# Attention edges of a graph network kernel: rows normalised on ScalarE, silu taken directly, one cross product over all channels, biases as a ones row, six filler products

## The chip, the cores and the metric

The kernel is one program on one core of a Trainium2 chip. The metric is the device time of a whole launch in microseconds (us), lower is better. The core has TensorE (PE: matmuls, with PEld its weight loads), VectorE (DVE), ScalarE (ACT), GpSimd (POOL) and SyncE (SP, which here only issues DMAs). Each engine runs its own instructions in the order in which they were written; engines wait for one another by semaphores. Everything is float32.

## The reference, cut to what matters

Three graph layers and a fourth with attention run on 100,000 nodes of 160 numbers (64 scalars and 32 vectors of 3) and 25,000 edges. The change lies in the part of the fourth layer that runs over the edges:

```
s, v = eq_ln(node)                      # rows of both ends of an edge, normalised
ms = s[src] @ msrc_ws + s[dst] @ mdst_ws + mdst_bs
mv = the same for the vectors
h  = silu(ln(edge_scalars @ rw1 + rb1, rg1, rbe1))      # radial network
h  = silu(ln(h @ rw2 + rb2, rg2, rbe2))
w1..w5 = split(h @ rw3 + roff)
Y1 = sqrt(3) * rhat                     # unit vector of the edge
ds = [w1 * ms, w4 * (mv . Y1) / sqrt(3)]
dv = [(w2 * ms) Y1, w3 * mv, w5 * cross(mv, Y1) / sqrt(2)]
ls, lv = ds @ lin_ws + lin_bs, dv @ lin_wv
alpha, values = first 64 of ls, (last 64 of ls, lv)
logit = sum over each head of smooth_leaky(alpha) * alpha_dot
```

Outputs of this part, for each edge: the logits (8 heads), the values (160), and the normalised row of its destination.

## The kernel before, in words

The program runs phases one after the other, with a barrier between: weights, all nodes, an edge index, three edge layers, `attention_weights`, `attention_edges` (L1653 to L2165), a softmax, and the destination nodes. Only `attention_weights` and `attention_edges` are changed.

`attention_edges` takes 25,000 edges in 25 rounds of 4 lanes; a lane holds J = 2 tiles of P = 125 edges (W = 250 columns when turned). There are thus 100 lane passes, and "a pass" below is the work of one lane, or the stretch of time in which each engine does each step once. Lane n owns the PSUM banks 2n and 2n+1.

The list `order` gives each step a position, `part` (17.05) the distance from lane to lane. `run_rounds` sorts the steps of the four lanes by position modulo 4 * part, and writes them for each engine in that order; so within a pass an engine's steps follow one another by position modulo `part`, and steps of three or four different edge lanes are interleaved. Nothing is reordered at run time.

The steps of a lane, in order of data: `load` (SP), `measure` to `widen` (DVE: statistics of the gathered rows), `roots` (POOL: a power, L1785), `divide` and `normalize` (DVE: L1868 to L1883), `turn_src`, `turn_dst` (PE transposes) with `copy_src`, `copy_dst` (ACT). Beside it the radial network, twice: `hidden` (PE), `h_add`, `h_measure`, `h_merge`, `h_widen` (DVE), `h_roots` (POOL, L1792), `h_normalize` (DVE), `turn_h` (PE), `activate` (ACT: the affine value and the tanh of half of it), `h_gate` (DVE: their product, a silu). Then `turn_vec`, `spread_vec` (PE) with ACT copies, `linear` (PE), `copy_linear` (ACT), `weights` (PE), `products`, `product4` (DVE), `outputs` (PE, 8 matmuls), `bias` (DVE), `copy_values`, `take_tanh` (ACT), `cross0` to `cross2` (DVE, 18 instructions of 32 elements, L1966), `leak`, `leaked`, `dot`, `add_heads` (DVE), `store` (SP). `keep_attr` (ACT) frees the row for `gather_next` (POOL): an index copy (L1761) and four indirect DMAs (L1768) that fetch the rows of the lane's next round.

`keep_busy0` to `keep_busy4` are steps of PE alone: 3, 2, 5, 3 and 3 matmuls of the identity (L127) whose results nobody reads. In the profile each float32 matmul leaves two records; so these 16 fillers are 32 records of L127 in a pass. A transpose leaves one record.

Of the kernel before, what the change touches and what calls it, by code (L numbers as in the profile page):

```python
# [7 lines left out]
ALU = mybir.AluOpType  # L8
# [5 lines left out]
P = 125  # L14
J = 2
# [1524 lines left out]
def attention_weights(nc, sem, keep, sb, banks, inp, w):  # L1540
# [45 lines left out]
    for name, src in (("lin_4", thrice(g["lin_ws"][S:S + U, :])),  # L1586
                      ("rb1", g["rb1"].unsqueeze(0).broadcast_to([P, 64])),
                      ("rb2", g["rb2"].unsqueeze(0).broadcast_to([P, 64])),
                      ("lin_b", g["lin_bs"].unsqueeze(0).broadcast_to([P, 128])),
                      ("alpha_dot", g["alpha_dot"].rearrange("h k -> (h k)").unsqueeze(0).broadcast_to([P, 64])),  # L1590
                      ("roff12", g["roff"][0:128].unsqueeze(1))):
        loads.append((w[name][:, :], src))
# [11 lines left out]
    with nc.Block() as block:  # L1604
# [6 lines left out]
        def _(v):  # L1611
            for x in ("src_s", "dst_s", "rw1", "rw2", "rw3", "proj_s", "spread"):
                v.memset(w[x][:, :], 0.0)
# [12 lines left out]
            kron(v, w["lin_5"], lin_5, 1.5 ** 0.5)  # L1626
            kron(v, w["proj_v"], proj_v, 1.0)
            v.tensor_copy(w["lin_a"][0:S, 0:128], lin_s[:, :])
            v.tensor_scalar(w["lin_a"][S:128, 128:160], lin_v0[S:128, :], 3 ** 0.5, None, ALU.mult)
# [3 lines left out]
            v.tensor_scalar(w["rw2"][0:64, :], rw2[:, :], 0.5, None, ALU.mult)  # L1633
            v.tensor_scalar(w["rw3"][0:64, 0:128], rw3[:, 0:128], 0.5, None, ALU.mult)
            for k in range(3):
                v.tensor_scalar(w["rw3"][0:64, 128 + k * V:128 + (k + 1) * V].rearrange("p (u c) -> p u c", c=3),
                                rw3[:, 128 + k * U:128 + (k + 1) * U].unsqueeze(2).broadcast_to([64, U, 3]),
                                0.5, None, ALU.mult)
            v.tensor_scalar(w["rg"][:, 2:4], w["rg"][:, 0:2], 0.5, None, ALU.mult)
            v.tensor_scalar(w["rbe"][:, 2:4], w["rbe"][:, 0:2], 0.5, None, ALU.mult).then_inc(built, 1)  # L1640
# [12 lines left out]
def attention_edges(nc, sem, sb, banks, inp, w, e, index, table, kept, logits, edges):  # L1653
# [7 lines left out]
    radial = [["h_added" + k, "h_measured" + k, "h_merged" + k, "h_widened" + k, "h_normed" + k, "h_gated" + k]  # L1661
              for k in ("1", "2")]
    t = lane_steps(sem, "att",
              pe=["attr_turned", "hidden1", "src_turned", "h_turned1", "dst_turned", "hidden2", "h_turned2",
                  "vec_turned", "vec_spread", "linear", "weights", "outputs"],
              act=["attr_copied", "src_copied", "h_activated1", "dst_copied", "attr_kept", "h_activated2",
                   "vec_copied", "spread_copied", "linear_copied", "values_copied", "tanh"],
              dve=["measured", "merged", "differences", "squares", "summed", "widened", *radial[0][:4], "x3",
                   "normed", *radial[0][4:], *radial[1], "products", "product4", "biased",
                   *[f"cross{k}" for k in range(3)], "leak", "leaked", "dotted", "logits"],  # L1670
              pool=["roots", "h_roots1", "h_roots2"])

    part = 17.05
    order = [("load", 0.0), ("turn_attr", 2.7), ("measure", 2.7), ("copy_attr", 3.3), ("merge", 4.25),
             ("differences", 4.95), ("hidden1", 5.2), ("squares", 5.4), ("add_squares", 5.65), ("widen", 5.85),
# [8 lines left out]
             ("copy_vec", 25.4), ("spread_vec", 26.0), ("keep_busy4", 26.46), ("copy_spread", 26.8),  # L1684
             ("linear", 27.4), ("copy_linear", 29.45), ("weights", 31.4), ("products", 33.45),
             ("product4", 34.9), ("outputs", 37.05), ("bias", 40.1), ("copy_values", 41.55),
             ("take_tanh", 41.95), ("cross0", 46.55), ("cross1", 47.75), ("cross2", 48.95), ("leak", 53.0),
             ("leaked", 53.35), ("dot", 53.65), ("add_heads", 55.2), ("store", 55.65)]

    fill = [(3, 1, 3), (1, 0, 2), (0, 0, 5), (0, 0, 3), (0, 0, 3)]  # L1690
# [4 lines left out]
    index_copied = [sem(f"att_index_copied_lane{n}") for n in range(LANES)]  # L1695
# [15 lines left out]
    h_u = sb("att_h_u", [64, LANES, W])  # L1711
    h_tanh = sb("att_h_tanh", [64, LANES, W])
    p5 = sb("att_p5", [V, LANES, W])
    keep = sb("att_keep", [P, T, KEPT + 1])
    alpha = sb("att_alpha", [P, LANES, J, 64])
    tanh = sb("att_tanh", [P, LANES, J, 64])
    logit = sb("att_logit", [P, T, HEADS])

    with nc.Block() as block:
        @block.sync  # L1720
        def _(sp):
# [3 lines left out]
            def load(n, i):  # L1725
# [3 lines left out]
                sp.wait_ge(t["dve"][n], count_at(t, i, "dve", "x3"))  # L1729
# [7 lines left out]
            def store(n, i):  # L1737
                sp.wait_ge(t["dve"][n], count_at(t, i + 1, "dve", "logits"))
                gate(sp, t)
                sp.wait_ge(t["act"][n], count_at(t, i + 1, "act", "attr_kept"))  # L1740
                gate(sp, t)
# [13 lines left out]
        def _(p):  # L1755
            prime(p, t, "pool")

            def gather(n, i):

                own = slice(J * n, J * n + J)  # L1760
                p.tensor_copy(e["ends_now"][:, :, own], index["ends"][:, :, bass.ds(i * T + J * n, J)]  # L1761
                              ).then_inc(index_copied[n], 1)
                p.wait_ge(index_copied[n], i + 1)
                gate(p, t)
# [7 lines left out]
            def gather_next(n, i):  # L1772

                p.wait_ge(gathered[n], 64 * i + 64)
                gate(p, t)
                p.wait_ge(t["dve"][n], count_at(t, i + 1, "dve", "normed"))
# [3 lines left out]
                gather(n, i + 1)  # L1780
# [14 lines left out]

            for n in range(LANES):
                gather(n, 0)
# [6 lines left out]
        def _(v):  # L1804
            for x in (e["attr_t"], e["h"], e["h2"], r_t):
                v.memset(x[:, :, :], 0.0)
            v.memset(keep[:, :, ATTR + 1:KEPT + 1], 0.0).then_inc(cleared, 1)
            prime(v, t, "dve")
# [54 lines left out]
            def divide(n, i):  # L1863

                v.wait_ge(t["pool"][n], count_at(t, i + 1, "pool", "roots"))
                v.wait_ge(kept_stored[n], 48 * i + 48)
                for j in range(J):
                    v.tensor_scalar(keep[:, J * n + j, X3:X3 + X], e["rows"][:, n, 1, j, 0:X],  # L1868
                                    e["rows"][:, n, 1, j, MEAN:MEAN + 1], root[:, n, 8 + j:9 + j], ALU.subtract, ALU.mult)
                    v.tensor_scalar(r[:, n, 0, j, :], e["y"][:, J * n + j, 0:3], root[:, n, 10 + j:11 + j], None,  # L1870
                                    ALU.mult)
                    ins = v.tensor_scalar(r[:, n, 1, j, :], e["y"][:, J * n + j, 0:3], root[:, n, 10 + j:11 + j],
                                          -1.0, ALU.mult, ALU.mult)
                one(ins, n)

            def normalize(n, i):
                for j in range(J):
                    for side, x in enumerate((e["xs"], e["xd"])):
                        k = side * J + j
# [758 lines left out]
```

## Time and profile before

| | |
|---|---|
| median of 3 runs | 11330.98 us (11328.65 to 11331.06) |
| the profiled execution, its own time | 11326.82 us |
| its span, first to last instruction | 11325.1 us |
| mean granted TensorE clock of the span | 0.88 of full |
| busy share of the span | PE 80%, PEld 73%, DVE 72%, ACT 40%, POOL 47% |
| `attention_edges` in the span | about 8122 to 10056 us |

Busy shares are averages over phases of different kinds; what bounds the changed phase is read in that phase. In the profile's rows a duration is that of one instruction from start to end; neighbours on an engine overlap a little, so the distance from start to start is shorter. PEclk 1.00 is the upper of the two clock levels of TensorE (2.4 GHz), 0.50 the lower (1.2 GHz).

### The profile page before, as it was taken

The numbers are of one execution on the slowest core, as the hardware profiler recorded it, in microseconds if no ns is written. First come the engines' busy times: TensorE is split into PE (matmuls) and PEld (weight loads), VectorE is DVE, ScalarE is ACT, GpSimd is POOL, SyncE is SP. The second block draws the span as 40 slices with busy tenths as digits, with TensorE's granted clock in tenths as the row PEclk, the third lists the DMA queues.
The fourth block names the chain that finished last, engine by engine and source line by source line (L and its number), as shares of the span: only waits on it lengthen the run. The fifth ranks groups of instructions, "written<-read, shape, count | busy, mean of one in ns | idle before, by whom it ended". The sixth has DMA issues, their size and how long they took to land. (4 is left out here: it accounts for less than half of the span.)

```text
span 11325.1 us, 241587 instructions
## 1 busy us (share of the span) xinstructions
PE 9089.1 (80%) x58771; PEld 8291.2 (73%) x58771; DVE 8098.2 (72%) x40535; ACT 4475.4 (40%) x17107; POOL 5279.8 (47%) x6680
## 2 busy tenths in 40 slices
PE   7877787777778787799978887888588888849998
PEld 6777777777777777688866676777577777738888
DVE  5666666666666666688878887888688888877777
ACT  4555555555555555333322232333222222212222
POOL 3444444444444444577755554555444444423444
PEclk8888888888888888899999998999888888869999
DMA  2222222222222222233322222222111111111111
GB/s 68 85 86 85 85 86 85 86 86 85 86 86 85 86 85 85 70 77 77 77 63 68 68 67 59 57 57 57 39 40 40 39 39 40 39 32 51 53 54 48
DMA packets 988491, 753.89 MB, mean 67 GB/s; under 512 B 430970, under 2 KB 948478, under 8 KB 988048
## 3 DMA queue, kind: packets, MB, share of 16 engines
q1 hardware_dynamic: 823696, 587.78, 18.4%
q0 software_dynamic: 164352, 162.20, 6.0%
q14 instruction: 409, 3.35, 0.1%
q8 instruction: 34, 0.56, 0.0%
HBM read 362.41 MB, written 392.80 MB: 67 GB/s over the span
## 5 line engine op out<-in xcount | busy, mean ns | idle before, releaser
L749 ACT ACTIVATE nodes_x<-nodes_z 125x161 f32<-125x161 f32 x2400 | 1005.5, 422 | 1439.1 <-DVE nodes_z L673 1437.4
L127 PE MATMUL bank<-ident 128*128 128x128 f32 x10000 | 1478.0, 297 | 97.1 <-PEq L883 58.7
L127 PEld LDWEIGHTS bank<-ident 128*128 128x128 f32 x10000 | 1415.1, 213 | 145.5 <-issue 59.2
L814 PE MATMUL bank<-self_v,nodes_v_t 128*125 128x98 f32 x4800 | 1153.2, 328 | 0.0
L812 PE MATMUL bank<-self_s,nodes_s_t 128*125 128x65 f32 x4800 | 977.2, 291 | 150.9 <-DVE ffn_y L233 143.6
L812 PEld LDWEIGHTS bank<-self_s,nodes_s_t 128*125 128x125 f32 x4800 | 879.8, 223 | 226.6 <-issue 206.4
L612 POOL TENSOR_SCALAR nodes_z<-nodes_sum 125x2 f32<-125x2 f32 x400 | 113.2, 283 | 1987.4 <-DVE nodes_sum L663 1987.4
L673 DVE SCALAR_TENSOR_TENSOR nodes_z<-bank,nodes_z 125x162 f32<-125x162 f32 x2400 | 811.2, 380 | 273.7 <-PE bank L814 271.4
L1203 POOL DMA_INDIRECT table<-edge_new,edge_into_now x600 | 733.5, 1222 | 565.5 <-issue 516.4
L312 PE MATMUL bank<-ident,ffn_sn 125*65 125x125 f32 x800 | 264.6, 346 | 788.3 <-DVE ffn_sn L214 784.3
L663 DVE TENSOR_REDUCE nodes_sum<-nodes_z 125x2 f32<-125x322 f32 x400 | 195.4, 489 | 948.8 <-DMA nodes_z<-rows 948.8
L814 PEld LDWEIGHTS bank<-self_v,nodes_v_t 128*125 128x125 f32 x4800 | 865.6, 226 | 0.0
L1171 POOL DMA_INDIRECT edge_rows<-table,edge_ends_now x416 | 519.6, 1249 | 598.0 <-DVE edge_carry L1056 532.2
L312 PEld LDWEIGHTS bank<-ident,ffn_sn 125*65 125x65 f32 x800 | 134.9, 169 | 839.1 <-issue 836.3
L1437 ACT ACTIVATE edge_sums<-bank 125x163 f32<-125x163 f32 x600 | 151.3, 304 | 1282.8 <-PE bank L1525 1282.8
L1171 POOL DMA_INDIRECT edge_rows<-rows,edge_ends_now x416 | 505.0, 1214 | 220.7 <-DVE edge_carry L1056 123.5
L1768 POOL DMA_INDIRECT att_edge_rows<-table,att_edge_ends_now x416 | 511.0, 1228 | 194.0 <-POOL att_edge_ends_now L1761 97.9
L233 DVE SCALAR_TENSOR_TENSOR ffn_y<-bank,nodes_z,nodes_u 125x160 f32<-125x160 f32 x800 | 270.3, 379 | 414.0 <-issue 220.1
L1288 DVE SCALAR_TENSOR_TENSOR edge_msg<-bank,edge_y,edge_msg 125x65 f32<-125x65 f32 x1800 | 510.0, 283 | 32.0
L795 PE MATMUL bank<-ident,nodes_z 125*65 125x125 f32 x1600 | 510.3, 334 | 1.4 <-DVE nodes_z L673 1.3
L796 PE MATMUL bank<-ident,nodes_z 125*97 125x125 f32 x1600 | 503.7, 331 | 0.0
L338 PE MATMUL bank<-f_v,ffn_hid_v 128*125 128x160 f32 x1600 | 478.3, 390 | 0.0
(496 smaller groups left out, 30563.3 us busy)
## 6 DMA issues: line engine op xcount, KB each, us to landing
table<-nodes_z SPq DMA_DIRECT2D x1200, 160.2 KB
nodes_z<-rows SPq DMA_DIRECT2D x400, 160.2 KB
out<-nodes_res SPq DMA_DIRECT2D x400, 156.2 KB
nodes_v_t<-x_t SPq DMA_DIRECT2D x400, 94.7 KB
edge_dst_row<-dst SPq DMA_DIRECT2D x300, 122.1 KB
ordered<-edge_new SPq DMA_DIRECT2D x200, 160.2 KB
edge_rows<-ordered SPq DMA_DIRECT2D x200, 160.2 KB
dest_rows<-kept SPq DMA_DIRECT2D x100, 316.4 KB
```

What stands on the lines that cost most here:

```text
L127: pe.matmul(banks[2 * ((n + lead) % LANES) + odd][:, 0:128], w["ident"][:, :], w["ident"][:, :], start=True, stop=True)
L338: ins = pe.matmul(b[0:P, o:o + F], f["hid_v2"][:, n, c], f["w"]["f2_v2"][:, :], start=False, stop=True, skip_group_check=True)
L673: ins = v.scalar_tensor_tensor(z[:, l + 1, k, 0:A + 1], banks[2 + n % 2][0:P, o:o + A + 1], z[:, l, k, A:A + 1], z[:, l, k, 0:A + 1], ALU. ...
L749: ins = act.activation(x3[:, k, :], z[:, l + 1, k, 0:X], ACT.Square, bias=z[:, l + 1, k, MEAN:MEAN + 1], scale=-1.0, accum_out=total[:, l, ...
L795: pe.transpose(banks[n % 2][0:S + 1, j * P:(j + 1) * P], z[:, l, k, 0:VS], ident)
L796: ins = pe.transpose(banks[n % 2][0:V + 1, W + j * P:W + (j + 1) * P], z[:, l, k, MEAN:X], ident)
L812: pe.matmul(banks[2 + n % 2][0:P, o:o + VS], xs[:, n, c], w[f"self_s{l}"][:, :], start=True, stop=True)
L814: ins = pe.matmul(banks[2 + n % 2][0:P, o + MEAN:o + A + 1], xv[:, n, c], w[f"self_v{l}"][:, :], start=False, stop=True, skip_group_check= ...
L1171: p.indirect_dma_start(e["rows"][:, n, side, j, :], None, source, bass.IndirectOffsetOnAxis(ap=e["ends_now"][:, side, k:k + 1], axis=0)).t ...
L1203: p.indirect_dma_start(target, bass.IndirectOffsetOnAxis(ap=e["into_now"][:, k:k + 1], axis=0), e["new"][:, n, j, :], None, bounds_check=n ...
L1288: v.scalar_tensor_tensor(scalars, bank[0:P, o:o + 1 + S], y, scalars, ALU.mult, ALU.add)
L1768: p.indirect_dma_start(e["rows"][:, n, side, j, :], None, table, bass.IndirectOffsetOnAxis(ap=e["ends_now"][:, side, k:k + 1], axis=0)).th ...
```

## The change

- `part` is 13.00 and every position in `order` is new. The fillers `keep_busy` go; instead `linear` issues six identity matmuls after its own four.
- `divide` and `normalize` of DVE become `offsets` on DVE (five small instructions: the unit vector with its first two components repeated, and minus mean times root for ten rows) and `normalize` on ACT: ten Identity activations with a bias and a scale per partition (four of 64, four of 96 and two of 161 columns).
- `activate` is one Silu instead of an Identity and a Tanh; `h_gate` goes. The radial bias becomes a row of ones in the operand and a row in the weights; `h_add` goes, and `h_measure` and `h_normalize` read PSUM.
- The output bias likewise; `bias` goes. `copy_values`, `take_tanh` and `cross0` wait for `outputs` itself. `outputs` has ten matmuls: a separate one of 32 columns, and one of 160 columns (5 per channel) in place of 96.
- The cross product: three multiplications and three additions over 125x192 elements (`cross0` to `cross3`) for 18 instructions. `leak` and `leaked` become one instruction.
- The index copy goes from POOL to ACT (`keep_attr`), with the wait for the gathered rows; `gather_next` is the four indirect DMAs.

```diff
-    part = 17.05
+    part = 13.00
+    order = [("load", 0.0), ("measure", 5.54), ("merge", 7.7), ("turn_attr", 9.71), ("copy_attr", 10.22),
+             ("differences", 10.3), ("hidden1", 10.63), ("squares", 10.87), ("h_measure1", 11.21),
+             ("add_squares", 11.46), ("widen", 11.68), ("roots", 11.9), ("offsets", 13.74), ("normalize", 14.31),
+             ("h_merge1", 14.36), ("h_widen1", 14.66), ("h_roots1", 14.9), ("h_normalize1", 15.66),
+             ("turn_h1", 16.16), ("activate1", 16.76), ("turn_src", 16.96), ("hidden2", 17.31),
+             ("copy_src", 17.61), ("h_measure2", 17.89), ("h_merge2", 18.3), ("h_widen2", 19.67),
+             ("h_roots2", 19.9), ("keep_attr", 20.08), ("gather_next", 20.52), ("turn_dst", 20.77),
+             ("copy_dst", 21.42), ("h_normalize2", 21.48), ("turn_h2", 22.04), ("activate2", 22.55),
+             ("turn_vec", 23.07), ("copy_vec", 23.58), ("spread_vec", 23.99), ("copy_spread", 24.6),
+             ("linear", 25.01), ("copy_linear", 26.54), ("weights", 27.23), ("products", 29.01),
+             ("product4", 30.38), ("outputs", 30.8), ("cross0", 32.75), ("cross1", 33.53), ("copy_values", 33.7),
+             ("take_tanh", 34.07), ("cross2", 34.3), ("cross3", 34.83), ("leak", 35.19), ("dot", 35.52),
+             ("add_heads", 35.84), ("store", 36.18)]
...
+            def offsets(n, i):
+                v.wait_ge(t["pool"][n], count_at(t, i + 1, "pool", "roots"))
...
+                v.tensor_tensor(r[:, n, :, 0:3], y[:, :, 0:3], scale.broadcast_to([P, J, 3]), ALU.mult)
+                v.tensor_tensor(r[:, n, :, 3:5], y[:, :, 0:2], scale.broadcast_to([P, J, 2]), ALU.mult)
+                v.scalar_tensor_tensor(offset[:, n, 0:4].unsqueeze(2), mom[:, n, 0, :, 0:1], -1.0,
+                                       root[:, n, 0:4].unsqueeze(2), ALU.mult, ALU.mult)
...
+            def cross0(n, i):
+                v.wait_ge(t["pe"][n], count_at(t, i + 1, "pe", "outputs"))
+                along, plus, minus = three(n)
+                v.tensor_tensor(along, vectors_of(n)[:, :, 0:U].unsqueeze(3).broadcast_to([P, J, U, 3]),
+                                turned_r(n, 0), ALU.mult)
+                v.tensor_tensor(plus, wide_of(n, 1), turned_r(n, 2), ALU.mult)
+                one(v.tensor_tensor(minus, wide_of(n, 2), turned_r(n, 1), ALU.mult), n)
...
             def activate(k):
                 def step(n, i):
                     wait("pe", n, i, f"h_turned{k + 1}")
-                    x = banks[2 * n + 1][0:64, 0:W]
-                    act.activation(h_u[:, n, :], x, ACT.Identity, bias=w["rbe"][:, k:k + 1],
-                                   scale=w["rg"][:, k:k + 1])
-                    one(act.activation(h_tanh[:, n, :], x, ACT.Tanh, bias=w["rbe"][:, 2 + k:3 + k],
-                                       scale=w["rg"][:, 2 + k:3 + k]), n)
+                    one(act.activation(e[("h", "h2")[k]][0:64, n, :], banks[2 * n + 1][0:64, 0:W], ACT.Silu,
+                                       bias=w["rbe"][:, k:k + 1], scale=w["rg"][:, k:k + 1]), n)
...
+            def normalize(n, i):
+                wait("dve", n, i, "offsets")
+                act.wait_ge(kept_stored[n], 48 * i + 48)
+                for j in range(J):
+                    for side, x in enumerate((e["xs"], e["xd"])):
+                        k, row = side * J + j, e["rows"][:, n, side, j, :]
+                        act.activation(x[:, n, j, 0:S], row[:, 0:S], ACT.Identity, bias=offset[:, n, k:k + 1],
+                                       scale=root[:, n, k:k + 1])
+                        act.activation(x[:, n, j, S:F], row[:, VS:X], ACT.Identity, bias=offset[:, n, 4 + k:5 + k],
+                                       scale=root[:, n, 4 + k:5 + k])
+                    ins = act.activation(keep[:, J * n + j, X3:X3 + X], e["rows"][:, n, 1, j, 0:X], ACT.Identity,
+                                         bias=offset[:, n, 8 + j:9 + j], scale=root[:, n, 8 + j:9 + j])
+                one(ins, n)
...
             def linear(n, i):
...
                 one(pe.matmul(a[0:V, W:2 * W], w["dst_v"][:, :], e["dv_t"][0:V, n, :], start=False, stop=True), n)
+                for _ in range(6):
+                    pe.matmul(banks[2 * n + 1][:, 0:128], w["ident"][:, :], w["ident"][:, :], start=True, stop=True)
...
-                    pe.matmul(bank[0:P, 0:160], e["p01"][:, n, c], w["lin_a"][:, :], start=True, stop=True)
...
+                    pe.matmul(heads[:, j, 0:128], e["p01"][:, n, c], w["lin_a"][:, :], start=True, stop=True)
+                    pe.matmul(heads[:, j, 0:128], p4[:, n, c], w["lin_4"][:, :], start=False, stop=True,
+                              skip_group_check=True)
+                    pe.matmul(heads[:, j, 128:224], e["p2"][:, n, c], w["lin_3"][:, :], start=True, stop=True)
+                    pe.matmul(vectors[:, j, 0:U], e["p01"][:, n, c], w["lin_sv"][:, :], start=True, stop=True)
+                    ins = pe.matmul(vectors[:, j, U:6 * U], p5[:, n, c], w["lin_5"][:, :], start=True, stop=True)
```

## Rows read from the trace of the kernel before

**Rows 1.** Windows, the loop of `attention_edges`: busy us (x instructions) per engine, PEclk, DMA.
```profile
8210.00:10010.00 1800.00, 1454.34 (x8612) 1289.46 (x8611) 1514.43 (x8404) 516.17 (x1632) 839.05 (x764) 0.84 0.18 39
```

**Rows 2.** Source line 1743, SP's store of a pass: ns min/median/max, first and last start.
```profile
L1743 SPq FUSED_REGOPS  x96: 37/51/74, 8225.0 to 10013.5; - x96
```

**Rows 3.** Timeline of POOL, one pass: start, us, engine, line, operation, [idle before].
```profile
9027.95 0.18 POOL L1761 COPY att_edge_ends_now<-edge_ends 125x4 int32 x1 [6.81 <-ACT att_keep L2030]
9029.08 1.28 POOL L1768 DMA_INDIRECT att_edge_rows<-table,att_edge_ends_now  x1 [0.95 <-POOL att_edge_ends_now L1761]
...
9034.91 0.75 POOL L1792 TENSOR_TENSOR att_h_root<-att_h_wide,half 125x2 f32<-125x2 f32 x1
9036.68 2.27 POOL L1785 TENSOR_TENSOR att_root<-att_wide,half 125x12 f32<-125x12 f32 x1 [1.02 <-DVE att_wide L1860]
...
9045.21 0.19 POOL L1761 COPY att_edge_ends_now<-edge_ends 125x4 int32 x1 [5.60 <-ACT att_keep L2030]
```

**Rows 4.** Lines of the phase, shapes apart, of ACT and DVE: busy us, mean ns.
```profile
L2015 ACT ACTIVATE att_h_u<-bank,att_rbe,att_rg 64x250 f32<-64x250 f32 x200 | 111.1, 556 | 766.4 <-PE bank L2105 766.4
L2009 ACT ACTIVATE att_edge_attr_t<-bank 64x250 f32<-64x250 f32 x100 | 37.3, 373 | 209.1 <-PE bank L2082 164.4 <-DVE att_keep L1807 44.6
L2050 ACT ACTIVATE att_keep<-bank 125x96 f32<-125x96 f32 x200 | 37.0, 237 | 7.2 <-DVE att_keep L1949 7.2
L1966 DVE SCALAR_TENSOR_TENSOR att_keep<-bank,att_r,att_keep 125x32 f32<-125x32 f32 x1800 | 322.7, 256 | 7.6 <-ACT att_keep L2050 0.5
L1882 DVE TENSOR_SCALAR att_edge_xs<-att_edge_rows,att_root 125x96 f32<-125x96 f32 x200 | 65.3, 327 | 0.0
L1891 DVE TENSOR_TENSOR att_hx<-bank,att_rb 125x128 f32<-125x128 f32 x200 | 56.2, 281 | 1.1 <-PE bank L2093 1.1
L1948 DVE TENSOR_TENSOR att_alpha<-bank,att_lin_b 125x64 f32<-125x64 f32 x200 | 43.7, 218 | 1.1 <-PE bank L2158 1.1
```

**Rows 5.** Timeline of ACT in the node phase: two Identity activations with bias and scale.
```profile
1007.09 0.93 ACT L759 ACTIVATE nodes_res<-ffn_y,nodes_out_offset,ffn_y_root 125x160 f32<-125x160 f32 x2
```

**Rows 6.** Timeline of all engines, one pass, parts of it.
```profile
9002.75 1.04 PE L2129 MATMUL bank<-att_r_t,att_spread 96*96 96x250 f32 x2
...
9010.26 0.48 DVE L1931 SCALAR_TENSOR_TENSOR att_edge_p<-bank,att_roff,att_edge_f 128x250 f32<-128x250 f32 x1 [1.27 <-PE bank L2148]
...
9012.48 0.51 PE L2154 MATMUL bank<-att_lin_a,att_edge_p 128*125 128x160 f32 x2 [1.66 <-DVE att_edge_p L1942]
...
9014.01 0.22 DVE L1825 BATCH_NORM_STATS2 att_stats<-att_edge_rows 125x6 f32<-125x64 f32 x1
...
9014.16 0.44 PE L2158 MATMUL bank<-att_lin,att_p 96*125 96x96 f32 x2
...
9015.46 0.18 DVE L1834 BATCH_NORM_AGGREGATE att_moments<-att_stats 125x2 f32<-125x6 f32 x1
...
9015.96 0.15 DVE L1835 BATCH_NORM_AGGREGATE att_moments<-att_stats 125x2 f32<-125x6 f32 x1
```

**Rows 7.** Timeline of PE, another pass, parts of it.
```profile
9036.53 0.37 PE L2105 MATMUL bank<-ident,att_hn 125*64 125x125 f32 x2 [2.67 <-DVE att_hn L1915]
...
9039.02 0.63 PE L2129 MATMUL bank<-att_r_t,att_spread 96*96 96x250 f32 x2
...
9042.80 0.84 PE L127 MATMUL bank<-ident 128*128 128x128 f32 x6
...
9044.03 0.59 PE L2145 MATMUL bank<-att_edge_h,att_rw 128*128 128x250 f32 x2
...
9046.11 0.62 PE L2093 MATMUL bank<-att_rw,att_edge_h 128*125 128x64 f32 x4 [0.23 <-DVE att_edge_h L1922]
```

**Rows 8.** Windows of three stretches after `outputs` of Rows 6; columns as in Rows 1.
```profile
9014.50:9018.00 3.50, 1.86 (x9) 1.56 (x8) 2.95 (x27) 0.00 (x0) 2.36 (x3) 0.50 0.26 64
9018.10:9020.90 2.80, 2.80 (x14) 2.60 (x15) 2.16 (x13) 1.47 (x5) 2.69 (x2) 0.50 0.45 110
9021.20:9026.00 4.80, 4.80 (x35) 4.35 (x33) 4.76 (x25) 1.83 (x6) 0.00 (x0) 1.00 0.09 13
```

More of the change, by code:

```diff
@@ L1660, in attention_edges @@
     logit_view = logits.rearrange("(t p) h -> p t h", p=P)
-    radial = [["h_added" + k, "h_measured" + k, "h_merged" + k, "h_widened" + k, "h_normed" + k, "h_gated" + k]
-              for k in ("1", "2")]
-    t = lane_steps(sem, "att",
[L1664 to L1671, printed above, removed]
@@ L1673, in attention_edges @@
-    part = 17.05
-    order = [("load", 0.0), ("turn_attr", 2.7), ("measure", 2.7), ("copy_attr", 3.3), ("merge", 4.25),
-             ("differences", 4.95), ("hidden1", 5.2), ("squares", 5.4), ("add_squares", 5.65), ("widen", 5.85),
[8 rows of a table removed]
[L1684 to L1688, printed above, removed]
@@ new lines, in attention_edges @@
+    done = {"pe": {"turn_attr": "attr_turned", "hidden1": "hidden1", "hidden2": "hidden2", "turn_src": "src_turned",
+                   "turn_dst": "dst_turned", "turn_h1": "h_turned1", "turn_h2": "h_turned2", "turn_vec": "vec_turned",
+                   "spread_vec": "vec_spread", "linear": "linear", "weights": "weights", "outputs": "outputs"},
+            "act": {"copy_attr": "attr_copied", "normalize": "normed", "copy_src": "src_copied",
+                    "copy_dst": "dst_copied", "activate1": "h_activated1", "activate2": "h_activated2",
+                    "keep_attr": "attr_kept", "copy_vec": "vec_copied", "copy_spread": "spread_copied",
+                    "copy_linear": "linear_copied", "copy_values": "values_copied", "take_tanh": "tanh"},
+            "dve": {"measure": "measured", "merge": "merged", "differences": "differences", "squares": "squares",
+                    "add_squares": "summed", "widen": "widened", "offsets": "offsets", "products": "products",
+                    "product4": "product4", "cross0": "cross0", "cross1": "cross1", "cross2": "cross2",
+                    "cross3": "cross3", "leak": "leaked", "dot": "dotted", "add_heads": "logits"},
+            "pool": {"roots": "roots", "h_roots1": "h_roots1", "h_roots2": "h_roots2"}}
@@ L1756, in _, with gather @@
             prime(p, t, "pool")
[L1758 to L1764, printed above, removed]
+            def gather(n):
                 for j in range(J):
@@ new lines, in cross1, with cross2, cross3 @@
+            def cross1(n, i):
+                after(i, n, "cross0")
+                along, plus, minus = three(n)
+                one(v.tensor_tensor(plus, plus, minus, ALU.subtract), n)
+            def cross2(n, i):
+                after(i, n, "cross1")
+                along, plus, minus = three(n)
+                one(v.tensor_tensor(plus, plus, along, ALU.add), n)
+            def cross3(n, i):
+                after(i, n, "cross2")
+                v.wait_ge(t["act"][n], count_at(t, i + 1, "act", "tanh"))
+                gate(v, t)
+                v.wait_ge(kept_stored[n], 48 * i + 48)
+                gate(v, t)
+                one(v.tensor_tensor(keep[:, J * n:J * n + J, S:F],
+                                    heads_of(n)[:, :, 128:224],
+                                    three(n)[1].rearrange("p j w c -> p j (w c)"), ALU.add), n)
@@ L1991, in _ @@
                 measure=measure, merge=merge, differences=differences, squares=squares, add_squares=add_squares,
-                widen=widen, divide=divide, normalize=normalize, **radial_steps("1"), **radial_steps("2"),
-                products=products, product4=product4, bias=bias, cross0=cross(0), cross1=cross(1), cross2=cross(2),
-                leak=leak, leaked=leaked, dot=dot, add_heads=add_heads))
+                widen=widen, offsets=offsets, **radial_steps("1"), **radial_steps("2"),
+                products=products, product4=product4, cross0=cross0, cross1=cross1, cross2=cross2, cross3=cross3,
+                leak=leak, dot=dot, add_heads=add_heads))
         @block.scalar
@@ L2028, in keep_attr @@
             def keep_attr(n, i):
-                wait("dve", n, i, "x3")
-                one(act.activation(keep[:, J * n:J * n + J, ATTR + 1:ATTR + 2], e["rows"][:, n, 1, :, A:A + 1],
-                                   ACT.Copy), n)
+                act.wait_ge(gathered[n], 64 * i + 64)
+                gate(act, t)
+                act.wait_ge(kept_stored[n], 48 * i + 48)
+                gate(act, t)
+                own = slice(J * n, J * n + J)
+                act.activation(e["ends_now"][:, :, own], index["ends"][:, :, bass.ds(i * T + T + J * n, J)], ACT.Copy)
+                one(act.activation(keep[:, own, ATTR + 1:ATTR + 2], e["rows"][:, n, 1, :, A:A + 1], ACT.Copy), n)
             def copy_vec(n, i):
@@ L2046, in copy_values @@
             def copy_values(n, i):
-                wait("dve", n, i, "biased")
-                for j in range(J):
-                    ins = act.activation(keep[:, J * n + j, S:F], banks[2 * n + j][0:P, 160:256], ACT.Copy)
-                one(ins, n)
+                wait("pe", n, i, "outputs")
+                one(act.activation(keep[:, J * n:J * n + J, 0:S], heads_of(n)[:, :, 64:128], ACT.Copy), n)
             def take_tanh(n, i):
-                wait("dve", n, i, "biased")
-                one(act.activation(tanh[:, n, :, :], alpha[:, n, :, :], ACT.Tanh, scale=0.5), n)
+                wait("pe", n, i, "outputs")
+                one(act.activation(tanh[:, n, :, :], heads_of(n)[:, :, 0:64], ACT.Tanh, scale=0.5), n)
             run_rounds(act, rounds, order, part, dict(
-                copy_attr=copy_attr, activate1=activate(0), activate2=activate(1),
+                copy_attr=copy_attr, normalize=normalize, activate1=activate(0), activate2=activate(1),
                 copy_src=copy_turned("src", e["s_t"], e["v_t"]), copy_dst=copy_turned("dst", e["ds_t"], e["dv_t"]),
```

188 lines of the change are left out of this document (83 added, 105 removed), and 8 rows, old and new, of the table order.

## The prediction

> **What bounds the kernel now.** I read the windows first, to see what the changed phase looks like inside. In its loop DVE is busy 1514 of 1800 us, PE 1454, POOL 839, ACT 516 [rows 1]. SP's stores give the length of a pass: (10013.5 - 8225.0) / 95 = 18.83 us [rows 2]. So DVE works 1514.43 / 1800 * 18.83 = 15.8 us of a pass and waits 3; it is the fullest engine, but not full. Of PE's 15.2, at least 4.5 are fillers whose results nobody reads (32 records at 0.84 / 6 = 0.14 at the upper clock [rows 7], more at the lower).
>
> Then I read the order of time, because on engines that run in a fixed order the pass can be as long as a ring of waits, with no engine full. In this phase there is one through POOL. The index copy waits for ACT's `keep_attr`, the four indirect DMAs and the radial root follow in a row, 9029.08 to 9034.91 to 9035.66 [rows 3]. At 9036.53 PE can turn `h2` after 2.67 us idle [rows 7]; then vector, spread, linear, `turn_dst`, ACT's copy and `keep_attr`, and the next index copy at 9045.21. From copy to copy that is 17.26 us, run wholly at the upper clock; the mean pass is 18.83, the difference being passes of which a part runs at the lower clock.
>
> That clock is the third thing to see. PE had been idle for 1.66 us before `outputs` (9012.48 [rows 6]); after `outputs` its clock is 0.50, stays there past another idle gap up to 9018, and is back at 1.00 by 9021.2 when PE has worked without a gap since [rows 8]. What it costs is seen on one step: `spread_vec` takes 1.04 us there [rows 6] and 0.63 otherwise [rows 7], 0.21 us for each record of 250 columns. The Trainium skill, "TensorE: Matmul & The Clock Gate", Part 1, says that the default state is throttled and activity releases it; it speaks against a change that takes fillers away, and by it alone the pass would not reach the sum at the upper clock. The trace agrees.
>
> **The engines after the change.** DVE loses all of `normalize` (eight instructions of up to 0.33 us), most of `divide`, both `h_add` (0.56), both `h_gate`, `bias` (four of 0.22), and for 3.2 us of `cross` (322.7 / 100) it gets six instructions of 192 elements. From 64 elements in 218 ns and 128 in 281, 192 take some 345 ns, started 0.28 apart: 1.7 us [rows 4]. Together DVE falls by about 6 us to 10. ACT gains ten activations. One with bias and scale pointers costs 556 - 373 = 183 ns more than a plain copy of the same shape [rows 4]; two of 160 columns take 0.93, so they start 0.41 apart [rows 5]; narrower ones are cheaper by about 0.9 ns a column (237 ns at 96 columns against 373 at 250, [rows 4]): 2 * 0.41 + 4 * 0.36 + 4 * 0.33 = 3.6 us. Less two activations of 0.46, ACT comes to about 8. POOL keeps 5.8 + 2.3 + 2 * 0.75 = 9.6 plus its waits. PE keeps at most 15.2 - 4.5 = 10.7, adds some 0.45 in `outputs` (four records at a sixteenth of the old step's 1.9 to 2.1 [rows 6]) and 1.7 of fillers: under 13. No engine is near 18.83; a ring must set the pass again.
>
> The Trainium skill, "ScalarE: Activation LUTs", Rules for kernel authors, wants multiplications and additions on VectorE, since ScalarE is slower at them. The row on L1882 agrees in direction: eight of at most 0.33 and two of about 0.36 on DVE are 2.6 to 3.3 us with overlap or without, against 3.6. By that rule alone this edit would lose up to 1 us a pass, where it stands on the ring below.
>
> **The gather ring (certain, if the order holds).** Reading the new order modulo 13.00: `gather_next`, then `roots` on POOL, `offsets` (DVE), `normalize` (ACT), `activate1` behind it on ACT, `hidden2` (PE), `h_measure2`, `h_merge2`, `measure`, `h_widen2` (DVE, in order), `h_roots2`, and the next `gather_next`. Each waits for the one before, by data or by its engine. Terms: gather 5.8 + 0.3 issue [rows 3]; `roots` 2.27 [rows 3]; `offsets` five tiny ones, priced by eight aggregates in 0.65 (9015.46 to 16.11 [rows 6]): 0.5, with 0.05 to wake; `normalize` 3.65; `activate1` 0.56 [rows 4]; `hidden2` 0.1 + 0.6 [rows 7]; `h_measure2` and `h_merge2` 0.7 (a fraction of `measure` and `merge`); `measure` 1.25 (9014.01 to at most 9015.46 [rows 6]); `h_widen2` 0.2, wake 0.2, `h_roots2` 0.75 [rows 3]. Sum 6.1 + 2.27 + 0.55 + 3.65 + 0.56 + 0.7 + 0.7 + 1.25 + 1.15 = 16.9 us. Uncertain are `normalize` (0.28 to 0.46 an activation: 2.8 to 4.6) and `offsets` (0.3 to 0.9): 15.9 to 18.3. The index copy with its 0.95 us of waiting (9027.95 to 9029.08 [rows 3]) is off this ring: on ACT it is 0.2 us beside other work.
>
> **The matmul ring.** `outputs`, `cross0`, `cross1`, `merge`, `cross2`, `h_normalize2` (DVE, in order), `turn_h2`, `activate2`, `turn_vec`, `copy_vec`, `spread_vec`, `copy_spread`, `linear`, fillers, `weights`, `products`, `product4`, `outputs`. At the upper clock: `outputs` 9012.48 to 9014.60, 2.1, with the new records 2.55 [rows 6]; DVE 0.05 + 0.9 + 0.3 + 0.6 + 0.3 + 0.6 = 2.8 (bound: 2.3 to 3.5); `turn_h2` 0.1 + 0.37 [rows 7], silu 0.56, wakes 0.15: 1.2; `turn_vec` 0.4, copy 0.37, wakes: 0.9; `spread_vec` 0.6 and its copy: 1.1; `linear` 1.6 (four matmuls like `weights`) and six fillers, twelve records at 0.84 / 6: 1.7 [rows 7]; `weights` 1.9 (9044.03 to 9046.11 less 0.23 idle [rows 7]); both products 9010.26 to 9012.48, 2.25 [rows 6]. Sum 2.55 + 2.8 + 1.2 + 0.9 + 1.1 + 3.3 + 1.9 + 2.25 = 16.0, under the gather ring. `copy_linear` (0.75) lies under the fillers; without them `weights` would wait about 1.1 for it, so of their 1.7 us 0.6 is on the ring.
>
> But before `turn_h2` PE is idle for 2.8 - 0.4 us, longer than the 1.66 that preceded a fall, then has only short steps with gaps until `linear`; nothing fills there any more. So I expect the lower clock from about `turn_h2` into `linear` in most passes: `turn_h2`, `turn_attr`, `turn_vec` and `hidden1` together 0.7 longer, `spread_vec` 0.4, and 1.3 of the 1.7 that `linear` could lose (8 records at 0.21). That makes 16.0 + 2.4 = 18.4 in such a pass.
>
> **Sum.** Two passes in three at 18.4 and one at 16.9 give 17.9 us. The method, applied to the kernel before, gives 17.3 at the upper clock against 18.83 in the mean, so a loss of this size to the clock is what was there. 99 passes at 18.83 - 17.9 = 0.93 save 92 us. The filling and emptying of the pipeline is one lane's latency, 55.65 / 17.05 = 3.26 passes of 18.83 before, 36.18 / 13.00 = 2.78 of 17.9 after, of which one is counted: 11 us less. Weights preparation: as many DMAs, a few DVE instructions, 0 (-2 to +3). The profiled execution took 11326.82, its span 11325.1: it would be 11224; the median is 4 above it: 11228 us.
>
> **Rivals.** (a) *The clock stays up*, because matmuls lie denser in a shorter pass. For it: a pass in which PE was idle 2.67 us kept 1.00 (9036.53 to 9046 run at upper-clock durations [rows 7]). Against it: ten fillers fewer. Then the gather ring sets 16.9: 99 * 1.93 + 13 = 204, 11127 us. (b) *Slower: the lower clock holds over `linear`, the fillers and into `weights`.* The fillers stand behind `linear`, so nothing raises the clock before it. `linear` then costs 1.7 more, the fillers 1.3, `weights` up to 0.8, with the 1.1 before: 16.0 + 1.1 + 3.0 to 3.8 = 20.1 to 20.9. It decides from 2.85 us over 16.0, which is 18.83; at a mixed 19.6 the cost is 76 - 8, 11399 us. (c) *The rings do not bind and the phase follows DVE and `part`*: 18.83 * 13.00 / 17.05 = 14.4, saving 99 * 4.47 + 17 = 460, 10871 us. For it: DVE was the fullest engine and loses 6 us. Against: 14.4 needs the gather ring 2.5 us shorter, and 5.8 + 2.3 of it are POOL instructions that are not changed. (d) *The gain is eaten exactly*, a pass between 18.6 and 19.05.
>
> **Chances.** My forecast (17.3 to 18.6) 0.50; (a) 0.22; (c) 0.07; (b) 0.12; (d) 0.09. No change is within 0.2%, 23 us, about what can be told apart here, or a pass of 18.7 to 19.2. Faster 0.80, same 0.08, slower 0.12. The range leaves out (c) and the far part of (b): 11085 (both rings a little cheaper than (a)) to 11350 us.
>
> **What would show it.** The stores 17.9 us apart; DVE near 10 us a pass; PE idle over 2 us before the transpose of `hn`; `spread_vec` and the first records of `linear` at the lower clock; mean clock of the loop below 0.84. The gather ring is right if POOL is idle only before the two radial roots, and `roots` starts right behind the fourth indirect DMA. `normalize` should take 3.6 us on ACT with `activate1` right behind. If `cross0` starts at once after `outputs`, but `turn_h2` doesn't wait for DVE, the matmul ring is wrong. A pass under 16 us would mean that the gather ring doesn't close.

## The result, and the profile after

The changed kernel took 11485.17 us (median of 3, 11482.97 to 11485.5) against 11330.98: ratio 1.0136, interval [1.0113, 1.0159]. It is slower, by 154 us, outside the range; the profiled execution took 11485.5 us, its span is 11483.4.

The windows and SP's store of the changed kernel (columns as in [rows 1, 2]):

```profile
8210.00:10010.00 1800.00, 1393.91 (x6510) 1089.39 (x6509) 873.65 (x5101) 730.95 (x2199) 755.61 (x616) 0.75 0.16 36
```

```profile
L1756 SPq FUSED_REGOPS  x96: 37/44/79, 8226.6 to 10172.1; - x96
```

A pass is (10172.1 - 8226.6) / 95 = 20.48 us, against 18.83 [rows 2]. These 95 passes take 157.0 us more than before, and the whole span is 158.3 us longer (11483.4 against 11325.1), so the loss lies in the pass. DVE fell as planned, 873.65 / 1800 * 20.48 = 9.9 us a pass against 15.8 [rows 1]; ACT rose to 8.3, and PE is busy 1393.91 / 1800 * 20.48 = 15.9 us of a pass. No engine is full, and PEclk is 0.75 where it was 0.84. So the time is in a ring of waits; PE's timeline shows it whole:

```profile
9100.69 0.46 PE L2176 MATMUL bank<-att_lin_a,att_edge_p 128*125 128x128 f32 x2 [0.69 <-DVE att_p L1935]
...
9103.38 0.27 PE L2136 MATMUL bank<-ident,att_edge_xd 125*96 125x125 f32 x1
9106.14 0.38 PE L2124 MATMUL bank<-ident,att_hn 125*64 125x125 f32 x2 [2.49 <-DVE att_hn L1914]
...
9107.25 0.37 PE L2143 MATMUL bank<-ident,att_r 125*3 125x125 f32 x2
...
9108.58 1.10 PE L2148 MATMUL bank<-att_r_t,att_spread 96*96 96x250 f32 x2
9110.23 1.17 PE L2155 MATMUL bank<-att_edge_s_t,att_src_s 65*128 65x250 f32 x2 [0.56 <-ACT att_spread_r L2056]
...
9113.70 2.77 PE L2160 MATMUL bank<-ident 128*128 128x128 f32 x12
9116.26 1.04 PE L2166 MATMUL bank<-att_edge_h,att_rw 128*128 128x250 f32 x2
...
9118.29 0.58 PE L2169 MATMUL bank<-att_edge_h,att_rw 128*96 128x250 f32 x2
...
9121.14 0.45 PE L2176 MATMUL bank<-att_lin_a,att_edge_p 128*125 128x128 f32 x2 [0.69 <-DVE att_p L1935]
```

On DVE between `outputs` and `turn_h2`, and at `products`:

```profile
9103.26 0.36 DVE L1950 TENSOR_TENSOR att_terms<-bank,att_r 125x192 f32<-125x192 f32 x1 [0.78 <-PE bank L2181]
...
9105.25 0.59 DVE L1914 TENSOR_SCALAR att_hn<-bank,att_h_moments,att_h_root 125x64 f32<-125x64 f32 x2
...
9118.91 0.48 DVE L1924 SCALAR_TENSOR_TENSOR att_edge_p<-bank,att_roff,att_edge_f 128x250 f32<-128x250 f32 x1 [4.61 <-PE bank L2169]
```

From one `outputs` (9100.69) to the next (9121.14) are 20.45 us. Each link below runs from the start of one step to the start of the next step of the ring, in us:

| link of the ring | predicted at the upper clock, us | measured, us |
|---|---|---|
| `outputs` to `cross0` (9103.26) | 2.55 | 2.57 |
| DVE, to `turn_h2` (9106.14) | 2.8 and 0.1 | 2.88 |
| to `turn_vec` (9107.25) | 1.1 | 1.11 |
| to `spread_vec` (9108.58) | 0.9 | 1.33 |
| to `linear` (9110.23) | 1.1 | 1.65 |
| to the fillers (9113.70) | 1.6 | 3.47 |
| to `weights` (9116.26) | 1.7 | 2.56 |
| to `products` (9118.91) | 1.9 | 2.65 |
| to `outputs` (9121.14) | 2.25 | 2.23 |

Everything off TensorE, and TensorE where its clock is up, is within 0.1 us of what was worked out; the other 4.4 us lie in the links whose matmuls run at the lower clock (`linear`: 1.04 us for two records that take 0.58 in `weights` once the clock is up). Windows of the idle gap, of the stretch after it and of the end of the pass show where it is:

```profile
9103.50:9106.00 2.50, 0.15 (x2) 0.00 (x0) 2.47 (x16) 0.83 (x4) 2.04 (x2) 1.00 0.08 8
9106.20:9117.80 11.60, 10.59 (x36) 7.94 (x37) 3.16 (x23) 5.53 (x16) 5.68 (x5) 0.56 0.27 61
9118.00:9123.00 5.00, 4.00 (x32) 3.43 (x30) 3.91 (x19) 1.52 (x6) 0.00 (x0) 1.00 0.00 0
```

The gather ring is not the bound here. POOL waits 9.41 us before the root of the second radial layer and gathers right after it:

```profile
9102.66 0.70 POOL L1798 TENSOR_TENSOR att_h_root<-att_h_wide,half 125x2 f32<-125x2 f32 x1 [9.41 <-DVE att_h_wide L1909]
9103.66 1.28 POOL L1776 DMA_INDIRECT att_edge_rows<-table,att_edge_ends_now  x1 [0.30 <-issue]
```

### The profile page after: what moved, and what is told of

It is laid out like the page before. It is cut to its first block and busy times, and to the rows that moved or that the text cites. A ratio compares the mean times of both kernels' runs of the same rounds, so it can differ in the third digit from the quotient of the medians.

```text
span 11483.4 us, 236806 instructions
## 1 busy us (share of the span) xinstructions
PE 9172.3 (80%) x57171; PEld 8204.5 (71%) x57171; DVE 7525.0 (66%) x37545; ACT 4767.4 (42%) x17907; POOL 5271.9 (46%) x6577
## 5 line engine op out<-in xcount | busy, mean ns | idle before, releaser
L127 PE MATMUL bank<-ident 128*128 128x128 f32 x6800 | 887.8, 278 | 96.6 <-PEq L883 58.7
L127 PEld LDWEIGHTS bank<-ident 128*128 128x128 f32 x6800 | 859.7, 194 | 123.5 <-issue 59.2
L1798 POOL TENSOR_TENSOR att_h_root<-att_h_wide,half 125x2 f32<-125x2 f32 x200 | 139.9, 700 | 1034.6 <-DVE att_h_wide L1909 1034.6
```

Of the source, the lines that this page charges most:

```text
L127: pe.matmul(banks[2 * ((n + lead) % LANES) + odd][:, 0:128], w["ident"][:, :], w["ident"][:, :], start=True, stop=True)
```

## The experiments

There are ten kernels; the times are medians. The kernel before took 11328 to 11330 us beside them. The pass lengths are from SP's store, as above, and PEclk is from windows that end before the loop does (before: 0.84, after the change: 0.75).

| kernel | us | ratio to before | pass us | PEclk in the loop |
|---|---|---|---|---|
| e1_fill_early | 11373.66 | 1.0039 [1.0025, 1.0053] | 19.39 | 0.76 |
| e2_no_fill | 11483.07 | 1.0135 [1.0118, 1.0152] | 20.48 | 0.67 |
| e3_fill_gaps | 11168.0 | 0.9858 [0.9842, 0.9875] | 17.25 | 0.97 |
| e4_hnorm_first | 11272.28 | 0.9949 [0.9933, 0.9966] | 18.35 | 0.78 |
| f1_gaps_hnorm | 11154.85 | 0.9845 [0.9828, 0.9861] | 17.23 | 0.91 |
| f2_gaps_widen | 11060.26 | 0.9764 [0.9748, 0.978] | 16.22 | 1.00 |
| f3_gaps_both | 10941.66 | 0.9659 [0.9643, 0.9676] | 15.03 | 0.99 |
| f4_gaps_norm_dve | 11305.34 | 0.998 [0.9971, 0.999] | 18.73 | 0.91 |
| g1_before_fill | 11701.76 | 1.0331 [1.0314, 1.0348] | 22.60 | 0.69 |
| g2_best_old_fill | 11268.51 | 0.9946 [0.993, 0.9963] | 18.35 | 0.78 |

**e1.** The six fillers of the changed kernel stand behind `turn_dst`, on a bank of the next lane.

```diff
             def linear(n, i):
-                for _ in range(6):
-                    pe.matmul(banks[2 * n + 1][:, 0:128], w["ident"][:, :], w["ident"][:, :], start=True, stop=True)
             def turn_rows(side, x):
+                    if side == "dst":
+                        for _ in range(6):
+                            pe.matmul(banks[2 * ((n + 1) % LANES)][:, 0:128], w["ident"][:, :], w["ident"][:, :], start=True, stop=True)
```

> The changed kernel with its six filler matmuls taken from behind linear and put behind turn_dst, where PE is idle 2.5 us. In the profile of the changed kernel a pass is 20.48 us, and the ring outputs, cross, h_normalize2, turn_h2, ..., linear, fillers, weights, products, outputs closes on it, with everything from turn_vec to the first half of weights at the lower clock. Theory A (the ring through the matmuls, lengthened by the lower clock): the fillers leave the ring, and the clock should be higher before linear. Pass 17 to 18 us if the clock is up by linear (total 11140 to 11240 us), 18.8 if it stays down (20.45 - 2.56 for the fillers + 0.9 for the wait that they covered; 11315 us). Theory B (the ring through POOL's gather and the ten new activations on ScalarE sets the pass): no change, 11485 us.

It is faster than the change by 112 us, so B falls. But the pass is 19.39 us, over both of A's figures. PE's timeline in this kernel:

```profile
9110.91 0.62 PE L2112 MATMUL bank<-att_rw,att_edge_attr_t 96*125 96x64 f32 x4
9111.39 1.06 PE L2151 MATMUL bank<-att_r_t,att_spread 96*96 96x250 f32 x2
9113.00 1.17 PE L2158 MATMUL bank<-att_edge_s_t,att_src_s 65*128 65x250 f32 x2 [0.56 <-ACT att_spread_r L2056]
...
9117.74 1.17 PE L2167 MATMUL bank<-att_edge_h,att_rw 128*128 128x250 f32 x2 [1.06 <-ACT att_edge_fv L2061]
```

The fillers only moved the low stretch later: `hidden1` runs at the upper clock again (0.62 us for 1.07), but `linear` and now all of `weights` at the lower. `spread_vec` is low in this pass but not in most: the median of its records in the loop is 0.42 us, that of the last records of `linear` and of `weights` 0.62. Of the 2.56 us of fillers that left the ring 1.06 came back as the wait for `copy_linear`. I had not thought that a few fillers can shift the fall instead of preventing it.

**e2.** The six fillers are deleted.

> The changed kernel without any filler. Theory A (clock): linear stays at the lower clock, the dense stretch that brings the clock back is shorter, so weights and outputs too run at the lower clock: 20.45 - 1.6 (fillers less the wait they covered) + 0.8 (weights) + up to 1.9 (outputs) = 19.6 to 21.6 us a pass, total 11400 to 11600 us. Theory C (the fillers hurt only by their own length on the ring, the clock is as it is): 18.8 us, 11315 us. Theory B (gather and ScalarE): no change, 11485 us.

The pass of 20.48 us is inside A's range; C's 18.8 is refuted. Fillers behind `linear` cost as much as they bring: with none or with six the pass is 20.48 us. The exchange can be read on two links of a pass: from `linear` to `weights` it is 1.20 us shorter (4.83 for 6.03), from `weights` to `outputs` 1.06 longer (5.94 for 4.88), since `weights` now runs wholly at the lower clock. That the mean lengths agree to 0.01 us isn't explained by this sum.

```profile
9108.04 1.17 PE L2155 MATMUL bank<-att_edge_s_t,att_src_s 65*128 65x250 f32 x2 [0.56 <-ACT att_spread_r L2056]
...
9112.87 1.17 PE L2164 MATMUL bank<-att_edge_h,att_rw 128*128 128x250 f32 x2 [1.16 <-ACT att_edge_fv L2061]
...
9118.81 0.45 PE L2174 MATMUL bank<-att_lin_a,att_edge_p 128*125 128x128 f32 x2 [0.49 <-DVE att_p L1935]
```

**e3.** There are 16 fillers, most of them in the gaps ahead of `linear`.

```diff
             def turn_rows(side, x):          # dst only; bank 2 * ((n + 1) % LANES)
+                        for _ in range(8): pe.matmul(banks[...][:, 0:128], w["ident"][:, :], w["ident"][:, :], ...)
             def turn_h(k):                   # k == "2" only; bank 2 * n, as in the next two
+                        for _ in range(1): ...
             def turn_attr(n, i):
+                for _ in range(1): ...
             def spread_vec(n, i):
+                for _ in range(2): ...
             def linear(n, i):
-                for _ in range(6):
+                for _ in range(4):
```

> The changed kernel with 16 fillers, as many as in the kernel before, put into PE's idle gaps: 8 behind turn_dst, 1 behind turn_h2, 1 behind turn_attr, 2 behind spread_vec, 4 behind linear. Theory A: the clock stays at its upper level over the pass, the matmul ring falls to about 15.5 us and the gather ring takes over at 16.9: total about 11124 us (11080 to 11200), granted clock of the loop over 0.95. Theory C (fillers only cost length): at best 18.8 us, 11315. Theory B with a gather ring longer than I worked out: no change.

The clock is up, 0.97 in the loop, and the pass is 17.25 us; the kernel is 317 us faster than the change and 162 faster than the kernel before. Number and place of the fillers changed together here; e1 changed only the place of six, which was worth 112 us. The ring that binds is now another one. The first fence is a window of one pass; the second shows POOL, which goes from gather into `roots` without a gap.

```profile
9104.80:9121.50 16.70, 13.31 (x92) 11.34 (x92) 9.52 (x58) 7.95 (x25) 8.63 (x7) 1.00 0.19 44
```

```profile
9110.89 1.31 POOL L1776 DMA_INDIRECT att_edge_rows<-table,att_edge_ends_now  x1 [0.45 <-ACT att_edge_dv_t L2038]
...
9115.52 1.21 POOL L1776 DMA_INDIRECT att_edge_rows<-table,att_edge_ends_now  x1 [0.30 <-issue]
9116.76 2.31 POOL L1791 TENSOR_TENSOR att_root<-att_wide,half 125x12 f32<-125x12 f32 x1
```

On PE, `turn_src` waits for the last of ScalarE's ten activations, as the gather ring says:

```profile
9106.32 0.29 PE L2140 MATMUL bank<-ident,att_edge_xs 125*65 125x125 f32 x1 [1.56 <-ACT att_keep L2030]
...
9109.90 0.27 PE L2141 MATMUL bank<-ident,att_edge_xd 125*96 125x125 f32 x1
9110.00 1.95 PE L2145 MATMUL bank<-ident 128*128 128x128 f32 x16
9112.75 0.38 PE L2126 MATMUL bank<-ident,att_hn 125*64 125x125 f32 x2 [0.79 <-DVE att_hn L1914]
```

**e4.** `("h_normalize2", 21.48)` becomes `20.0`.

> The changed kernel with one position changed: h_normalize2 runs on VectorE behind cross0 instead of behind cross1, merge and cross2. Theory A: 1.5 us (cross1 0.28, merge 0.6, cross2 0.28 and their waits) leave the matmul ring and PE's idle time before turn_h2 falls from 2.5 to 1.0 us: 18.9 us a pass with the clock as it is (11325 us), down to 17.2 (11155 us) if the shorter gap keeps the clock up. Theory B: no change, 11485 us.

The pass is 18.35 us, 2.13 less: 1.5 of DVE and some of the clock, between A's two figures. PEclk in the loop is 0.78 for 0.75: the clock still falls before `linear` (its matmuls take 1.04 us here too).

**f1.** This is e3 with the edit of e4, and with 4 fillers instead of 8 behind `turn_dst`.

> The kernel of e3_fill_gaps (fillers in the gaps) with h_normalize2 moved ahead of cross1 as in e4_hnorm_first, and 4 instead of 8 fillers behind turn_dst, since the gap there is 1.5 us shorter. In e3_fill_gaps a pass was 17.25 us. Theory A1 (with the clock up, the gather ring sets the pass): shortening the matmul ring changes nothing: 17.2 us, 11165 us within 20. Theory A2 (the matmul ring still sets it): 1.5 us less, 15.7 us, 11010 us. If four fillers are too few to keep the clock: above 11200 us.

It is A1: 11154.85 us, 13 less than e3 and within 20 of the 11165 expected. What was worth 213 us at the lower clock is worth almost nothing once the other ring binds. With four fillers fewer the clock of the loop fell from 0.97 to 0.91, and the pass (17.23 us) did not grow by it.

**f2.** This is e3 with `("h_widen2", 19.67)` at `18.5`.

> The kernel of e3_fill_gaps with h_widen2 moved on VectorE ahead of measure (position 18.5). Theory A1 (gather ring): measure's 1.25 us leaves the ring; 16.0 us a pass, where the matmul ring at the upper clock, 15.5 us, is next: 11040 us (11020 to 11090). Theory A2 (matmul ring): no change, 11168 us.

The pass is 16.22 us, 1.03 less, as A1 says. Shortening one link of the gather ring shortens the pass, so that ring is what binds in e3.

**f3.** These are f1 and f2 together, with the two widest activations in a step of their own:

```diff
             def normalize(n, i):
...
-                    ins = act.activation(keep[:, J * n + j, X3:X3 + X], ...)
+            def keep_row(n, i):          # at 17.8, behind copy_src at 17.61
+                act.wait_ge(kept_stored[n], 48 * i + 48)
+                for j in range(J):
+                    ins = act.activation(keep[:, J * n + j, X3:X3 + X], ...)
```

> Both moves, and the two activations of 161 columns (the kept destination rows) taken out of normalize into a step of their own behind copy_src. Gather ring 17.2 - 1.25 - 0.83 = 15.1 us, matmul ring 15.5 - 1.5 = 14.0 us: 15.1 us a pass, about 10950 us (10930 to 11050). If the clock falls with 12 fillers: up to 11150 us. Should be the best version so far, under both kernels.

The pass is 15.03 us for an expected 15.1 and the time 10941.66 us for 10950: 389 us under the kernel before, 544 under the change.

**f4.** This is e3 with `normalize` on VectorE behind `h_widen1`: the ten activations as `tensor_scalar(..., ALU.mult, ALU.add)` with root and offset pointers.

> The kernel of e3_fill_gaps with the ten normalising instructions on VectorE (one multiply and add with two pointers each) behind h_widen1 instead of on ScalarE. Theory R (the ring decides): 2.6 to 3.3 us of VectorE work now stand before h_normalize1 and products, on the ring by gather, roots, offsets, products, product4, h_measure2, h_roots2: 18.3 us a pass, 11275 us (11200 to 11330). Theory S (VectorE is the faster engine for such work, and it has 9 us to spare): 1 us shorter than on ScalarE, 16.2 us, 11065 us.

The pass is 18.73 us in the mean, 1.48 more than on ScalarE; the time, 11305.34 us, is inside R's range. DVE's timeline in this kernel:

```profile
9106.05 0.17 DVE L1880 TENSOR_TENSOR att_r<-att_edge_y,att_root 125x6 f32<-125x6 f32 x1 [5.79 <-issue]
...
9106.91 0.32 DVE L1895 TENSOR_SCALAR att_edge_xs<-att_edge_rows,att_root,att_offset 125x64 f32<-125x64 f32 x1
...
9109.04 0.35 DVE L1899 TENSOR_SCALAR att_keep<-att_edge_rows,att_root,att_offset 125x161 f32<-125x161 f32 x1
9109.31 0.59 DVE L1928 TENSOR_SCALAR att_hn<-bank,att_h_moments,att_h_root 125x64 f32<-125x64 f32 x2
9109.82 0.47 DVE L1938 SCALAR_TENSOR_TENSOR att_edge_p<-bank,att_roff,att_edge_f 128x250 f32<-128x250 f32 x1
```

The ten take 2.4 us there, from 9106.91 to 9109.31; on ScalarE in e3 they take 3.6 (below). VectorE is the faster engine for them, and the kernel is slower. On VectorE they stand in front of `h_normalize1` and `products`, on ScalarE beside them, so S's gain of 1 us is refuted. But R is not shown to be the whole cause. The starts of `roots` around this pass lie 17.04, 22.58, 18.50 and 17.03 us apart, and this pattern comes back round after round. Two passes in four are thus no longer than in e3 and shorter than R's 18.3. The long one begins where VectorE stands idle for 5.79 us, put down to "issue" and not to a wait, and starts `offsets` 2.9 us after `roots` has ended (9103.15). The trace has 23 such stops in 25 rounds, 133.3 us together; in e3 `offsets` waited for `roots` all 100 times. Why they come is open.

**g1.** This is the kernel before without `keep_busy`, with the six fillers behind `linear`.

> The kernel before with one part of the change alone: its keep_busy steps (16 fillers) go, and six fillers stand behind linear. Theory A: at the upper clock the ring of the kernel before (17.26 us) changes little (-1.35 for fillers that leave it, +1.7 for the six), but the clock falls before linear and stays low over linear and fillers: 20 to 21 us a pass against 18.83, 11450 to 11550 us. So this part alone would make up the whole loss. If the fillers' place doesn't matter: 17.6 to 18.8 us, 11210 to 11330 us.

The pass is 22.60 us, 1.6 beyond the longest that was expected, and that rest is not accounted for. PE is idle 2.71 us before `turn_h2`, and the gaps behind it are open as well:

```profile
9115.48 0.60 PE L2105 MATMUL bank<-ident,att_hn 125*64 125x125 f32 x2 [2.71 <-DVE att_hn L1915]
9117.26 0.57 PE L2124 MATMUL bank<-ident,att_r 125*3 125x125 f32 x2 [1.19 <-ACT att_h_tanh L2017]
9118.38 1.12 PE L2129 MATMUL bank<-att_r_t,att_spread 96*96 96x250 f32 x2 [0.55 <-ACT att_r_t L2035]
9120.06 1.17 PE L2136 MATMUL bank<-att_edge_s_t,att_src_s 65*128 65x250 f32 x2 [0.56 <-ACT att_spread_r L2039]
```

The other three matmuls of `linear`, right behind these rows, take 1.04 us each, where 0.58 is their length at the upper clock. This part alone costs 374 us (against the 11327.57 measured beside it), more than the whole change; the rest of the change gives 217 back (11701.76 to 11485.17).

**g2.** This is f3 with the fillers of the change.

> The kernel of f3_gaps_both (10942 us) with the fillers of the change: six behind linear, none elsewhere. Its two edits on the gather ring should then be worth nothing, since the matmul ring at the lower clock binds, as in e4_hnorm_first (11272 us, 18.35 us a pass): 11272 us within 30. If the clock is not what separates them, it stays near 10942 us.

It takes 11268.51 us, within 4 us of e4: two links taken off the gather ring are worth nothing while the other binds. The fillers alone, twelve mostly in the gaps against six behind `linear`, are worth 327 us here; how much of that is their place and how much their number, no run separates.

## Why the prediction was wrong

- **The matmul ring was found and right.** Its links at the upper clock sum to 16.0 us, no link off TensorE is more than 0.1 us off, and taking 1.5 us out of it shortened the pass of the changed kernel by 2.13 (e4).
- **The step that failed** is "`spread_vec` 0.4, and 1.3 of the 1.7 that `linear` could lose ... 18.4 in such a pass". Measured against the table: `linear` lost 1.87 us for the 1.3 put, the fillers 0.86 and `weights` 0.75, for both of which I had put nothing, the short steps with `hidden1` and `spread_vec` 1.0 for 1.1: together 4.4, not 2.4. I let the clock come back in the middle of `linear`; it came back within `weights`. It also fell later than I said: `turn_h2` (0.38) and `turn_vec` (0.37) still ran at the upper clock, `hidden1` (1.07) no longer.
- **"Two passes in three"** was wrong as well: over 95 passes the mean is 20.48 us, no shorter than the pass shown, in which the whole stretch from `hidden1` into `weights` is low. The rows over all passes say the same: a record of the last matmul of `linear` takes 0.62 us in the mean, its length at the lower clock, and one of the third matmul of `weights`, of the same 250 columns, 0.37, its length at the upper. So the clock falls and rises at nearly the same place of each pass. That this is because the idle gap and the sparse steps behind it are the same each time is argued, not tested.

```profile
L2158 PE MATMUL bank<-att_edge_dv_t,att_dst_v 96*96 96x250 f32 x200 | 104.0, 624 | 0.0
L2168 PE MATMUL bank<-att_edge_h,att_rw 128*96 128x250 f32 x200 | 58.5, 374 | 0.0
```

- **Rival (b) was what happened,** and its own figures, 20.1 to 20.9 us, hold 20.48. I gave it 0.12 and then priced it at "a mixed 19.6". Of its terms only the fillers were far off (1.3 for 0.86). The argument that decides it stood in its text: nothing raises the clock before `linear`. (a) was argued from one pass that kept 1.00 after an idle gap of 2.67 us; but there eleven fillers followed `turn_h2`, `turn_vec` and `spread_vec`, and those were the ones taken away.
- **The gather ring, 16.9,** was right though hidden: 17.25 in e3; 16.22 for 16.0 in f2 and 15.03 for 15.1 in f3, both worked out from e3's measured pass. `normalize` was 3.6 us as priced: in e3 the ten start at 9102.49 and `activate1` follows at 9106.08, right behind the last of them. The first two rows are ACT's in e3, the other two those of the first and the last of the ten in the changed kernel:

```profile
9102.49 0.44 ACT L2026 ACTIVATE att_edge_xs<-att_edge_rows,att_offset,att_root 125x64 f32<-125x64 f32 x1 [0.81 <-DVE att_offset L1886]
...
9106.08 0.54 ACT L2015 ACTIVATE att_edge_h<-bank,att_rbe,att_rg 64x250 f32<-64x250 f32 x1
```

```profile
9114.57 0.43 ACT L2026 ACTIVATE att_edge_xs<-att_edge_rows,att_offset,att_root 125x64 f32<-125x64 f32 x1
...
9117.73 0.51 ACT L2030 ACTIVATE att_keep<-att_edge_rows,att_offset,att_root 125x161 f32<-125x161 f32 x1
```

- **DVE from 15.8 to 10, ACT to 8, no engine full:** right. PE, priced under 13, was busy 15.9 us a pass, for the same reason as the rest: its records took longer at the lower clock. (c), that the phase follows DVE, is refuted: DVE lost 5.9 us and the pass grew by 1.65.
- **The gain of the arithmetic** is there once the clock is: e3 is 162 us faster than the kernel before. In the changed kernel it was turned into low-clock time on TensorE.

## What to carry to other kernels

When engines are emptied in a kernel with a fixed order, add up the rings of waits, each link from a row. Then ask at which clock each TensorE link will run after the change. A filler is worth what it does to the steps behind it: here six of them gained 112 us by moving from behind the long matmuls into the idle gap ahead of them (e1), and that was not enough to keep the clock up. Shorten the ring that binds, and expect nothing from the other until it does (e4 and g2, f1 and f2). Where an instruction stands on a ring can count for more than how fast its engine is: ten instructions that VectorE does in 2.4 us and ScalarE in 3.6 gave no shorter pass on VectorE (f4). Read more than one pass before a mean is put down to a ring: in f4 one pass in four was the long one.

## What the hardware showed that I had not expected

- Six fillers in the largest gap did not keep the clock up but moved its fall into the longer matmuls (e1: `linear` and `weights` low, 0.76 in the loop). 16 spread over the pass gave 0.97 in a pass of 17.25 us (e3) and 1.00 in one of 16.22 (f2); 12 gave 0.91 in one of 17.23 (f1) and 0.99 in one of 15.03 (f3). How many are needed, and whether as many behind `linear` would do the same, was not tried.
- Passes were 20.48 us long with six fillers and with none, and 18.35 in both e4 and g2. The second pair has the same matmul ring; for the first no cause is shown.
